# Loading the second weight matrix of each expert once instead of twice, at an address that TensorE reads from a register

## The reference

```python
logits = xt @ Wr + br
top_p, top_idx = jax.lax.top_k(softmax(logits), 2)
h = act(jnp.einsum('end,edh->enh', xe, W1) + b1[:, None, :])
y = jnp.einsum('enh,ehd->end', h, W2) + b2[:, None, :]
out = (weights[:, :, None] * take_along_axis(y, top_idx)).sum(axis=1)
```

## Time and profile before

| | us |
|---|---|
| median of 3 runs | 3862.68 (3856.25 to 3864.88) |
| profiled execution | 3858.63 |
| its span | 3857.0 |
| TensorE busy | 2515.6 (65%) |
| GpSimd busy | 2247.8 (58%) |
| VectorE busy | 1421.5 (37%) |
| ScalarE busy | 1407.3 (36%) |
| mean granted TensorE clock | 0.824 of full |

### The profile page before, as it was taken

The page is one execution under the profiler, slowest core; times in us unless marked ns, Lnnn a source line. Parts: engine busy times, 40 slices in busy tenths (PEclk is TensorE's granted clock), DMA queues, the critical chain, the costliest instruction groups (busy, mean ns, idle before and its releaser), DMA issues. The chain is left out here.

```text
span 3857.0 us, 51256 instructions
## 1 busy us (share of the span) xinstructions
PE 2515.6 (65%) x11978; PEld 1714.0 (44%) x12059; DVE 1421.5 (37%) x4194; ACT 1407.3 (36%) x3611; POOL 2247.8 (58%) x2388
## 2 busy tenths in 40 slices
PE   0156654999999960787404666666666663399990
PEld 0122221555555540776403444444444443389990
DVE  4169995333332231000294444444443444000003
ACT  0038884343441020232105444444444432255550
POOL 0458887777777705776437777777777752200005
PEclk9989998999999965898756667666667766699995
DMA  2554344666665513778427777777777742442213
GB/s 101 184 183 114 110 115 128 187 188 196 191 199 184 181 49 143 238 242 263 158 67 231 207 201 208 202 205 206 203 205 203 205 111 109 144 166 79 78 35 102
DMA packets 333459, 628.87 MB, mean 163 GB/s; under 512 B 85723, under 2 KB 179877, under 8 KB 330583
## 3 DMA queue, kind: packets, MB, share of 16 engines
q0 software_dynamic: 123408, 356.51, 30.7%
q1 hardware_dynamic: 207047, 269.82, 22.2%
q10 hardware_dynamic: 2848, 0.79, 0.1%
HBM read 448.65 MB, written 179.90 MB: 163 GB/s over the span
## 5 line engine op out<-in xcount | busy, mean ns | idle before, releaser
L598 POOL DMA_INDIRECT agg_r_rows<-h_table,b_src x856 | 857.8, 1002 | 322.9 <-issue 215.1
L647 PE MATMUL agg_r_sums<-agg_r_rows,agg_r_onehot 128*128 128x257 f32 x1712 | 706.2, 562 | 380.6 <-DVE agg_r_rows L619 330.1
L647 PEld LDWEIGHTS agg_r_sums<-agg_r_rows,agg_r_onehot 128*128 128x128 f32 x1712 | 430.9, 275 | 640.0 <-issue 575.4
L1172 PE MATMUL ly_low<-parts,matrix 128*128 128x512 bf16 x1794 | 599.6, 380 | 0.0
L1173 PE MATMUL ly_high<-parts,matrix 128*128 128x256 bf16 (+1 forms) x1875 | 513.3, 274 | 37.6 <-PEq L112 33.1
L619 DVE TENSOR_TENSOR agg_r_rows<-agg_r_rows,agg_r_rel 128x514 f32<-128x514 f32 x428 | 299.1, 699 | 642.5 <-DMA agg_r_rows<-h_table,b_src 640.1
L1374 POOL DMA_INDIRECT rl_buf<-r_table,rl_kind x408 | 395.0, 968 | 151.1 <-issue 117.5
L565 ACT ACTIVATE agg_r_gap<-iota,b_near 128x128 f32<-128x128 f32 x856 | 295.1, 392 | 505.0 <-PE agg_r_sums L647 473.9
L1841 PE MATMUL f_pH<-f_xT,f_w 128*128 128x128 f32 x2816 | 362.9, 289 | 73.3 <-DMA f_w<-in_L_ffn_w 57.6
L1841 PEld LDWEIGHTS f_pH<-f_xT,f_w 128*128 128x128 f32 x2816 | 349.9, 203 | 100.0 <-issue 67.6
L1909 DVE TENSOR_TENSOR f_yb<-f_pY,f_b 128x256 f32<-128x256 f32 x120 | 51.0, 425 | 898.0 <-PE f_pY L1853 898.0
(11 more groups left out here) (359 smaller groups left out, 3205.7 us busy)
## 6 DMA issues: line engine op xcount, KB each, us to landing
agg_r_rel<-relation_rows SPq DMA_DIRECT2D x428, 260.0 KB, 3.1
relation_rows<-rl_buf POOLq DMA_DIRECT2D x204, 260.0 KB, 2.7
f_w<-in_L_ffn_W SPq DMA_DIRECT2D x28, 1024.0 KB, 5.6
relation_rows<-f_rr_buf POOLq DMA_DIRECT2D x88, 260.0 KB, 3.5
relation_rows<-rr_buf POOLq DMA_DIRECT2D x80, 260.0 KB, 2.7
f_w<-in_L_ffn_w SPq DMA_DIRECT2D x38, 512.0 KB, 5.7
f_xb<-f_xs SPq DMA_DIRECT2D x122, 128.0 KB, 2.0
f_xs<-f_zero SPq DMA_DIRECT2D x15, 1024.0 KB, 9.6
```

Source lines behind the costliest of these rows:

```text
L598: pool.indirect_dma_start(rows[:, n % SLOTS, t, :], None, table, bass.IndirectOffsetOnAxis(ap=indices[:, t:t + 1], axis=0)).then_inc(s_row ...
L647: last = nc.tensor.matmul(sums[:, n % BANKS, 0:used], onehot[:, n % BANKS, t, :], rows[:, n % SLOTS, t, 0:used], start=t == 0, stop=t == 1)
L1172: nc.tensor.matmul(low[:, n % 2, :], m[:, s, own], of[:, s, 0:2 * D], start=s == 0, stop=s == NT - 1)
```

## The change

`e_tab` gets two more rows. Row 2 is 1 for each tile that is the first of its expert, row 3 the parity of the expert's running number, both worked out by VectorE at the end of `route`. SP loads W2 only at the first tile of an expert, into the slot `room` given by row 3, and the results of all of the expert's tiles read it there. W1 stays as it was, with `fresh` and the slot s. SP therefore reads four values for each tile instead of two, and TensorE reads one, `room`, ahead of each result, and takes the address of its moving operand from it.

```diff
-        e_tab = k.sb(f"{name}_etab", [1, 2, tiles], I32)
+        e_tab = k.sb(f"{name}_etab", [1, 4, tiles], I32)
...
+        turn, order, zeros = (k.sb(f"{name}_{x}", [1, tiles]) for x in ("turn", "order", "zeros"))
...
                 v.tensor_tensor(e_tab[:, 1, 2:tiles], done_f[:, 2:tiles], done_f[:, 0:tiles - 2], ALU.not_equal)
                 v.memset(e_tab[:, 1, 0:2], 1)
+
+                v.memset(turn[:, 0:1], 1.0)
+                st.link(v.memset(zeros[:, :], 0.0))
+                st.link(v.tensor_tensor(turn[:, 1:tiles], done_f[:, 1:tiles], done_f[:, 0:tiles - 1], ALU.not_equal))
+                v.tensor_copy(e_tab[:, 2, :], turn[:, :])
+                st.link(v.tensor_tensor_scan(order[:, :], turn[:, :], zeros[:, :], 0.0, ALU.add, ALU.add))
+                st.link(v.tensor_copy(e_tab[:, 3, :], order[:, :]))
+                v.tensor_scalar(e_tab[:, 3, :], e_tab[:, 3, :], 1, None, ALU.bitwise_and)
...
                     ax = xs[bass.ds(t * P + P, P), :]
+                    first = sp.value_load(e_tab[0:1, 2, bass.ds(t, 1)], min_val=0, max_val=1)
+                    room = sp.value_load(e_tab[0:1, 3, bass.ds(t, 1)], min_val=0, max_val=1)
 
                     sp.wait_ge(s_h, t * HB + HB)
                     weights(sp, fresh, w1b[:, s, :, :], a1, s_w1[s])
...
                     sp.wait_ge(s_y, t + 1)
-                    weights(sp, fresh, w2b[:, s, :, :], a2, s_w2[s])
+                    weights(sp, first, w2b[:, bass.ds(room, 1), :, :].rearrange("p a k d -> p (a k) d"), a2, s_w2[s])
...
                 def result(t, s, u):
+                    room = pe.value_load(e_tab[0:1, 3, bass.ds(t, 1)], min_val=0, max_val=1)
 
                     pe.wait_ge(s_w2[s], u * 16)
                     pe.wait_ge(s_yb, t + 1)
                     for f in range(FC):
 
                         pe.wait_ge(s_hT, t * FC + f + 1)
-                        last = nc.tensor.matmul(pY[s][:, 0:D], hT[:, s, f, :], w2b[:, s, f, :], start=f == 0, stop=f == FC - 1)
+                        last = nc.tensor.matmul(pY[s][:, 0:D], hT[:, s, f, :], w2b[:, bass.ds(room, 1), f, :].rearrange("p a d -> p (a d)"), start=f == 0, stop=f == FC - 1)
```

## The result

The changed kernel takes 3921.42 us at the median of 4 runs (3912.01 to 3937.22), beside 3863.78 us for the kernel before (3856.25 to 3876.91): 1.015 times as long, 95% interval 1.0105 to 1.0194. The forecast was 3920.5 us, and the single runs of the changed kernel lie 25 us apart. A second set of the two gave 3925.61 against 3864.87 us, 1.0135 (1.0104 to 1.0166). The changed kernel is slower.

A forecast was written before the change was run, and what follows sets the result against it. It took TensorE to bound f1 and a closed loop of x load, turn, result and store f0. 38 + 16 - 7 + 11 = 58 us raised 3858.63 to 3916.6, the median to 3920.5; range 3885 to 3965.

The forecast's parts named there:

- The closed loop of x, turn, result, store: f0: each x load waits, through store and result, for an earlier turn; 8.54 us per two tiles, period growing to 5.24.
- nothing in it is spare: f0: SP waits 0.8 us a tile for results, yet the loop was said to leave no slack for added reads.
- rival E: About 0.8 us of SP's waiting per tile is spare; pair costs 16 us, loads win 16: 3863 us, chance 0.07.
- SP's pair, 42 us in f0: f0: two added SP reads take 1.3 us a pair, half counted in each of 64 tiles.
- the term for the tiles around changes of expert: f0, about 24 tiles, start included: SP's pair delays w1's issue, 0.66 us each, 16 us.
- TensorE's read, 12 us: f0, about 40 tiles: TensorE's read between turn and result is exposed, 0.6 us in the two-tile loop; hidden in f1.
- The rival that hid it (3908.5 us): Rival B: TensorE's reads are hidden in f0 too, so 12 us drop out; chance 0.12.
- The removed loads, 7 us won: f0: 5 to 8 w2 loads go, each worth 1.1 us; nothing won in f1.
- f1, 10.6 us: f1: w1 of the first tile after a change of expert comes 1.3 us later, about 8 such delays.
- Address steps and the seven operations in route: Address steps on TensorE cost nothing while its lead lasts, otherwise 0.1 us per result; route's VectorE operations hidden, otherwise 2 us a stage.
- The rival of a lower clock (3958 us): Rival C: new gaps in f0 lower TensorE's clock for 4 of 10 tiles, 36 to 40 us more; chance 0.13.
- SP's own list at 4.8 us a tile: f0: SP's own work with the added pair stays below the new period of 5.24 us, so adds nothing more.

The follow-up runs named there:

- e2: The kernel before plus one unused TensorE table read ahead of each result: 3884.55 us, ratio 1.0062.
- e1: The kernel before plus two unused SP table reads per tile, where the change has its own: 3899.07 us, ratio 1.0135.
- e4: The changed kernel with SP's two new reads moved behind the x load: 3894.2 us, ratio 1.0115.
- e9: The kernel before with SP's two values read by one load, a tile ahead, behind the x load, without range check: 3992.64 us, ratio 0.9931 in a slower set.
- e3: The changed kernel with the removed w2 loads put back into a buffer that nobody reads: 3936.38 us, ratio 1.0221.
- e5b: The changed kernel with TensorE's read moved ahead of the turn: 3915.44 us, ratio 1.0131.
- e8: The changed kernel with SP's four reads a tile ahead and unchecked, TensorE's read ahead of the turn: 4001.31 us, ratio 0.9958 in a slower set.
- e10: The changed kernel with SP's four values read by one early, unchecked load, TensorE's read ahead of the turn: 3997.33 us, ratio 0.9933 in a slower set.

## Why the prediction was right

The direction and the two causes, a pair of reads on SP and one on TensorE, were right. That the forecast missed by 1 us is luck: three of its terms were off and cancel, and in the profiles the change took 66.5 us where the terms made 58.

*The closed loop of x, turn, result, store.* Right in the main. With both engines' reads the period came out at 5.29 to 5.57 us, where 5.24 was forecast, and SP still waits 0.5 us a tile in the changed kernel (6.5 us in 70), so its list doesn't explain that period; e2 shows a delay on TensorE coming back as a later x. Not right is "nothing in it is spare". Of the 1.3 us that the pair adds to each tile SP's waits took about half, 13.2 us in 70 falling to 1.8 (e1). The 0.8 us a tile also stands on a wrong reading. The 16.6 us of the earlier trace rows contain one wait of 6.3 us that began at 1572.3, before the clean stretch, and leave out 7.0 us of waits for VectorE's add; 10.3 + 7.0 us in 21 tiles happens to give 0.8 again. And rival E divides by two once too often: a list with 0.8 us of room in each tile would grow by 0.5 us a tile, 32 us in 64 tiles, which is as much as e1's f0 showed. By the size of e1 alone E isn't refuted; the changed kernel's period is what it can't give.

*SP's pair, 42 us in f0.* Right in kind, too large: 31.9 us. What failed is the term for the tiles around changes of expert, 24 tiles and 16 us. In tiles 48 to 60 the pair costs nothing where it stands (91.4, 91.0 and 91.7 us in before, e1 and changed); in the other 52 tiles e1 grew by 32.3 us, 0.62 each, as the sum has it. Moving the pair later gained 9.7 us in tiles 48 to 60 (e4); why adding it is free there and moving it away pays isn't settled, and e9, which moved its reads too and gained nothing there, speaks against the place alone.

*TensorE's read, 12 us.* Right that it is exposed in f0 and hidden in f1, too small: 19.9 us (e2). The read delays a result by 0.75 us where its turn waited (0.97 instead of 0.22), where 0.6 was taken, and each tile of the clean stretch grew by 0.45 us instead of 0.3. It also cost something outside the 40 tiles for which it was counted. The rival that hid it (3908.5 us) falls. The Trainium skill, in the opening table of TensorE: Matmul & The Clock Gate, gives that engine's queue 64 entries. That the sequencer therefore runs far ahead was the prediction's own inference; f1 fits it, where the read lies 1.9 us ahead of its matmul, and f0 doesn't, where the read starts 0.1 us after the turn that waited.

*The removed loads, 7 us won.* Not found: nothing that can be told from zero (e3, 399.4 us between 397.7 and 402.5). A reason that fits, but that no run tests, is that the long register reads and the late x stand beside w1's loads as well, and those all remain. There were 5 fewer in f0, at the lower end of the 5 to 8 counted. The three terms of f0 made 38 + 16 + (-7) = 47 us; measured one by one they are 31.9 + 19.9 + 0 = 52, and the change showed 50.2.

*f1, 10.6 us.* Right: 9.6 us by the stretch from its fourth tile (418.5 against 408.9), 7.1 of it from the pair alone (e1), nothing from TensorE's read (408.0); the remaining 2.5 us have no run of their own. The w1 wait went from 1.20 to 2.46 us as forecast, and the second tile doesn't wait. e4 gives it back (409.1).

*Address steps and the seven operations in route.* Nothing from route: f0's first turn comes 110.4 us after route's first VectorE instruction before, and 111.0 after. Of the 8.1 us by which f0 starts later, 7.5 are there when route begins, by that first instruction's row in either trace:

```profile
L1653 DVE MEMSET f_zero<- x2: 1765/1765/1765, 1436.3 to 3223.9; 128x2048 f32 x2
```

```profile
L1654 DVE MEMSET f_zero<- x2: 1765/1765/1765, 1443.8 to 3280.9; 128x2048 f32 x2
```

Nothing ahead of that point was changed. Starts of f0 in the first and third set lie from 1546.6 to 1556.8 us, those of kernels built on the changed one mostly late in that range and one of them at 1548.5; a cause wasn't found. The address steps weren't measured alone, but they can be seen: in the changed kernel the result that starts at 1607.19 has one more register step right ahead of its first weight load, and results come 1.10 and 1.17 us after a turn that waited, against 0.97 in e2.

```profile
L1865 PEldq FUSED_REGOPS  x1: 51/51/51, 1607.1 to 1607.1; - x1
```

So the "some 0.1 us per result" that the prediction kept for the case without a lead is, by estimate from these two figures, what shows in f0; its sum had it at nothing.

*The clock.* The rival of a lower clock (3958 us) falls: 1.00 in the clean stretch with TensorE busy 55 of 70 us.

*What the forecast didn't see* is the second limit: it put SP's own list at 4.8 us a tile, below the period, and so at no cost. That is true of the changed kernel, by some 0.5 us a tile (6.5 us of waiting in 70), but the room is small, and both repairs ran out of it (e4, e5b).

## What to carry to other kernels

Ask of every instruction that is put on a queue whether that queue is part of a closed loop, by following one item around it in the timeline, and not by the queue's busy share or its waits: SP waited 0.8 us a tile, and 1.3 us more a tile still cost half of themselves. Then add up the queue's whole list too. Out of the loop a read of 0.65 us with its tests was free only while that list was shorter than the period, which e4 and e8 show by what they didn't gain. So read early, read together, and leave a transfer alone that nobody waits for. On TensorE a read was hidden where the sequencer was ahead (f1) and not behind a turn that waited for its data (f0).

## What the runs showed of the hardware

One load of several neighbouring values costs little more than one of a single value, but not in each form. SP's loads in f1, four values of a tile (e10), then two values (e9):

```profile
L1804 SPq TENSOR_LOAD <-f_etab x39: 295/299/307, 3502.6 to 3793.5; - x39
```

```profile
L1795 SPq TENSOR_LOAD <-f_etab x39: 463/472/477, 3505.7 to 3794.4; - x39
```

One value takes 263 ns at the median in f1 of the changed kernel:

```profile
L1807 SPq TENSOR_LOAD <-f_etab x55: 261/263/269, 3391.3 to 3817.4; - x55
```

That two take longer than four wasn't expected; the entries lie 8 bytes apart in one table and 16 in the other, and no run separates count from spacing. The Trainium skill, in DMA: Bandwidth & Descriptors, section Latency and other measured facts, gives a `tensor_load` a floor of about 600 ns. The trace doesn't agree: medians of 263 and 299 ns for one and four values in f1, both well below that. Single loads took up to 1397 ns in f0, with the weight and relation traffic beside them:

```profile
L1802 SPq TENSOR_LOAD <-f_etab x62: 263/337/1397, 1562.5 to 1942.5; - x62
```
